# Normalised tiles 3 and 4 transposed by DMA in 16-bit halves, in a gated cross-attention and mixture kernel

## The reference

```
xn = layernorm(x)
x  = x + tanh(g_x) * (fake_quant(xn) @ fake_quant(ctx[b]))      # per batch b, ctx[b] is 1024 x 1024
z  = layernorm(x)                                               # "ln" in the kernel
gate = softmax(z @ W_gate.T);  thr = sigmoid(z @ W_thr + b_thr) * 0.125
w  = relu(gate - thr), divided by its sum
h  = z @ A_w.T                                                  # (rows, 8, 16)
x  = x + tanh(g_f) * (z @ W_base.T + b_base + 2 * (h * w) @ B_w)
```

## Time and profile before

| | us |
|---|---|
| median of 3 runs | 184.81 (184.8 to 185.39) |
| the profiled execution, its own time | 184.05 |
| its span, first to last instruction | 182.3 |

### The profile page before, as it was taken

The page is one execution under the profiler, slowest core; times in us unless marked ns, Lnnn a source line. Parts: engine busy times, 40 slices in busy tenths (PEclk is TensorE's granted clock), DMA queues, the critical chain, the costliest instruction groups (busy, mean ns, idle before and its releaser), DMA issues.

```text
span 182.3 us, 2890 instructions
## 1 busy us (share of the span) xinstructions
PE 172.4 (95%) x1052; PEld 149.9 (82%) x1058; DVE 111.9 (61%) x281; ACT 90.6 (50%) x123; POOL 72.0 (39%) x89
## 2 busy tenths in 40 slices
PE   4868999989999999999899999999999999999993
PEld 4755446678989999999764479999999999999993
DVE  0999985989678987968863563392451351351313
ACT  2389923575986936193910106142890880820300
POOL 3461023931001396199888887036400500500220
PEclk9999999999999999999999999999999999999999
DMA  6999999999130332065050000005309207102003
GB/s 210 318 381 386 386 410 406 362 395 387 62 117 0 112 118 119 0 117 174 0 169 7 0 0 0 4 0 101 129 0 150 84 0 171 61 4 115 2 0 115
DMA packets 19934, 25.39 MB, mean 139 GB/s; under 512 B 11207, under 2 KB 12615, under 8 KB 19920
## 3 DMA queue, kind: packets, MB, share of 16 engines
q1 hardware_dynamic: 19906, 25.21, 41.8%
q10 hardware_dynamic: 14, 0.00, 0.0%
HBM read 18.39 MB, written 4.19 MB: 124 GB/s over the span
## 4 chain that ended last, share of the span: by engine, by line
PE 76%; DVE 11%; DMA 4%; ACT 4%; issue 4%; POOL 0%; DVEq 0%; ACTq 0%
PE bank L1042 16%; PE bank L1044 16%; PE bank L1043 15%; PE bank L920 14%; PE bank L1002 3%; DVE st L661 3%; DVE q L696 2%; DMA q1T<-q 2%; PE bank L1066 2%; PE bank L978 2%; DMA xs<-in_x_dram 2%; PE bank L1068 2%; PE bank L1067 2%; DVE lnTl L729 1%; PE bank L1030 1%
## 5 line engine op out<-in xcount | busy, mean ns | idle before, releaser
L1042 PE MATMUL bank<-WTh,lnTh 128*128 128x388 f32 (+3 forms) x192 | 67.3, 350 | 0.3 <-DVE lnTl L729 0.3
L1044 PE MATMUL bank<-WTh,lnTl 128*128 128x388 f32 (+3 forms) x192 | 65.1, 339 | 0.0
L1043 PE MATMUL bank<-WTl,lnTh 128*128 128x388 f32 (+3 forms) x192 | 65.0, 339 | 0.0
L1042 PEld LDWEIGHTS bank<-WTh,lnTh 128*128 128x128 f32 x192 | 36.2, 188 | 1.2 <-DVE lnTl L729 0.6
L1043 PEld LDWEIGHTS bank<-WTl,lnTh 128*128 128x128 f32 x192 | 36.2, 189 | 0.3
L1044 PEld LDWEIGHTS bank<-WTh,lnTl 128*128 128x128 f32 x192 | 36.2, 188 | 0.3
L437 POOL TENSOR_TENSOR xs<-xs,tb 128x1024 f32<-128x1024 f32 x8 | 19.2, 2404 | 39.6 <-ACT xs L491 39.6
L920 PE MATMUL bank<-q,q1T 128*128 128x512 bf16 x122 | 29.1, 379 | 0.8 <-DVE q L696 0.5
L431 POOL TENSOR_TENSOR xs<-xs,colbc 128x512 f32<-128x512 f32 x14 | 18.0, 1309 | 15.9 <-DVE xs L715 11.1
L920 PEld LDWEIGHTS bank<-q,q1T 128*128 128x128 bf16 x128 | 12.1, 98 | 14.3 <-DVE q L696 0.6
L661 DVE BATCH_NORM_STATS2 st<-xs 128x6 f32<-128x512 f32 x32 | 20.7, 682 | 4.2 <-DMA xs<-in_x_dram 4.2
(11 more groups left out here) (102 smaller groups left out, 230.8 us busy)
## 6 DMA issues: line engine op xcount, KB each, us to landing
xs<-in_x_dram SPq DMA_DIRECT2D x8, 512.0 KB, 7.2
landing<-in_ctx_dram SPq DMA_DIRECT2D x8, 512.0 KB, 10.9
ring<-in_ctx_dram SPq DMA_DIRECT2D x8, 512.0 KB, 6.6
out_dram<-xs SPq DMA_DIRECT2D x7, 512.0 KB, 2.9
ring<-in_L_ffn_W_base_dram SPq DMA_DIRECT2D x4, 512.0 KB, 12.7
landing<-in_L_ffn_W_base_dram SPq DMA_DIRECT2D x4, 512.0 KB, 15.4
ring<-in_L_ffn_A_w_dram SPq DMA_DIRECT2D x1, 512.0 KB, 12.5
ring<-in_L_ffn_B_w_dram SPq DMA_DIRECT2D x1, 512.0 KB, 5.9
```

The costliest lines, as they stand in the source:

```text
L1042: mm(o, hi, WTh[:, k, a:b], start=(k == 0), stop=False, skip_group_check=True)
L1043: mm(o, hi, WTl[:, k, a:b], start=False, stop=False, skip_group_check=True)
L1044: ins = mm(o, lo, WTh[:, k, a:b], start=False, stop=(k == KT - 1), skip_group_check=True)
```

## The change

Tiles 3 and 4 are taken into `by_dma`: they are no longer transposed by TensorE but by DMA in halves. For tile 3 the transposed halves lie in `colbc`, which is free between the transposes of B and batch 1's column term, since slot 4 of the ring still holds ctx. Its `halve` stands behind `normalise(3)` in tile 1, its DMA ahead of batch 1's q1 transposes on SP, its join and high part behind the last ctx copies in tile 2, its low part among batch 1's additions. `halve(4)` stands behind `normalise(4)`. For tiles 4 to 7 the join stands behind the split of hw; before, it stood ahead of that split. The added wait in `transpose_ln`, for `flipped` of the second half of B, keeps the DMA off `colbc` until the transposes of B are done.

```diff
-    by_dma = [t for t in range(T) if t > MT]
+    by_dma = list(range(MT - 1, T))
...
-        halvesT = ring[:, 4, :].bitcast(U16).rearrange("p (b t) -> p b t", t=P)
+        def halvesT(t):
+            return (colbc[:, :] if t < MT else ring[:, 4, :]).bitcast(U16).rearrange("p (b t) -> p b t", t=P)
...
@@ SP, transpose_ln
                 if n:
                     sp.wait_ge(ln_joined, n)
-                sp.dma_start(halvesT, halves, transpose=True).then_inc(ln_transposed[t], 16)
+                else:
+                    sp.wait_ge(flipped, flip_no["B", 0, 1] + 1)
+                sp.dma_start(halvesT(t), halves, transpose=True).then_inc(ln_transposed[t], 16)
@@ SP, loop over t
                     if t + 3 == A1_AFTER:
+                        transpose_ln(MT - 1)
                         transpose_q1(MT)
                         transpose_q1(MT + 1)
                         transpose_q1(MT + 2)
                     if t + 2 == A1_AFTER:
                         transpose_q1(MT + 3)
-                    if t + 3 in by_dma:
+                    if t + 1 == A1_AFTER:
+                        transpose_ln(MT)
+                    if t + 3 in by_dma and t + 3 > MT:
                         transpose_ln(t + 3)
@@ ScalarE, loop over t
                 if t + 1 == MT:
                     normalise(MT)
+                    halve(MT)
...
-                if t + 1 in by_dma:
-                    join(t + 1)
-                elif t + 1 < T:
+                if t + 1 not in by_dma and t + 1 < T:
                     split_hi(("ln", t + 1, 0))
                     split_hi(("ln", t + 1, 1))
                 if t + 1 == A1_AFTER:
                     affine_ctx(CPB + 5)
                 split_hi(("hw", t, 0))
-                if t + 1 in by_dma:
+                if t + 1 in by_dma and t + 1 >= MT:
+                    join(t + 1)
                     joined_hi(t + 1)
...
-                if t + 2 in by_dma:
+                if t + 2 in by_dma and t + 2 != MT:
                     halve(t + 2)
...
                 if t + 1 == A1_AFTER:
                     affine_ctx(CPB + 6)
                     affine_ctx(CPB + 7)
+                    join(MT - 1)
+                    joined_hi(MT - 1)
                     scale_columns(1, 0)
                     scale_columns(1, 1)
@@ VectorE
                 split_lo(("hw", t, 0))
-                if t + 1 in by_dma:
+                if t + 1 in by_dma and t + 1 >= MT:
                     joined_lo(t + 1)
...
                     add_product(1, 0, 3)
+                    joined_lo(MT - 1)
                     add_product(1, 1, 0)
```

More of the change, by code:

```diff
@@ L536, in join @@
                 nc.scalar.copy(lnT.bitcast(U16).rearrange("p (c h) -> p h c", h=2),
-                               halvesT.rearrange("p (h k) t -> p h (k t)", h=2)).then_inc(ln_joined, 1)
+                               halvesT(t).rearrange("p (h k) t -> p h (k t)", h=2)).then_inc(ln_joined, 1)
             def joined_hi(t):
```

## The result

The changed kernel takes 190.54 us (median of 5 runs, 190.05 to 190.69) where the kernel before, run beside it, took 184.81: a ratio of 1.0302, 95% interval 1.0281 to 1.0322. Forecast were 189.6, in 187.8 to 191.2. The profiled execution, the fastest of the five, took 190.05 us with a span of 188.2, 5.9 above the span before.

What follows compares the result with a forecast made beforehand. TensorE, busy 95% of the span, bounds the kernel. Terms 0.0 + 3.25 + 0.74 + 0.74 = +4.7 us on the profiled 184.05 give 188.8; plus 0.76 for the median and 0.1 for first products, 189.6 us, range 187.8 to 191.2.

Steps and rivals of the forecast that it cites:

- tile 3 in sum: Tile 3 by DMA: -0.68 us for transposes gone from TensorE, +0.7 for q1's later landing, together 0.0.
- hw of tile 4 late: VectorE's moments wait behind tile 4's low part, so TensorE transposes hw of tile 4 2.51 us later than before.
- from there to tile 5: From hw of tile 4 to tile 5's first product: 5.48 us through the join instead of 4.74, +0.74.
- tile 6: Start of tile 6: TensorE waits for the join behind the split of hw, +0.74 us.
- tile 7: Start of tile 7: TensorE waits for the join behind the split of hw, +0.74 us.
- the queue on SP: Tile 3's transpose ahead of q1's on SP makes q1's data land late: 0.7 us taken, bounds 0 and 1.9.
- Tile 4's landing: DMA of tile 4's halves, issued at 112.1, lands before its join can start at 117.0, hidden by 0.1 to 0.7 us.
- the estimate set beside the sum: At some 275 ns per TensorE transpose, tile 4's eight would give back 2.2 us, whole sum about +3.3 us.
- The clock rival: TensorE's clock halves from the stop before hw of tile 4 to that tile's end: 194.3 us, chance 0.04.
- The rival of the joins alone: Only the late joins at tiles 4 to 7 cost, late moments being hidden: +2.1 us, 186.9 us, chance 0.06.
- the faster one: Join chain fits under 4.74 us and moments come under 1.28 us late: -1.55 us, 183.3 us, chance 0.04.
- The one of q1's transpose waiting out tile 3's: q1's data starts only after tile 3's landing, 2.1 us late: +6.1 us, 190.9 to 191.5 us, chance 0.10.

Runs made afterwards that it cites:

- experiment 2: Changed kernel with the join of tiles 5 to 7 ahead of the split of hw again, tile 4's join left behind it: 188.70 us.
- experiment 1: Changed kernel with VectorE's moments of tiles 5, 6 and 7 moved ahead of tile 4's low part: 187.62 us.
- experiment 4: Changed kernel with tile 4 back on TensorE and the joins of tiles 5 to 7 ahead of the split of hw: 185.01 us.
- experiment 6: Changed kernel with tile 3's DMA transpose issued on SP behind the q1 transposes of tiles 4 to 6: 189.97 us.
- experiment 7: Changed kernel, moments and joins of tiles 5-7 earlier, tile 3's transpose behind q1's, 16 idle start matmuls, earlier ctx rounding: 184.33 us; only tile 3 by DMA: 183.53.
- experiment 9: Kernel before with 16 idle start matmuls and earlier ctx rounding: 183.84 us; beside it, only tile 3 by DMA with all edits: 183.59 us.
- experiment 8: Changed kernel with 16 instead of 6 idle matmuls at its start: 189.91 us.
- experiment 3: Changed kernel with both the moments ahead of tile 4's low part and the join of tiles 5 to 7 ahead of hw's split: 185.06 us.

## Why the prediction was right

Against the spans of the two profiled executions, step by step in us:

| step | forecast | measured | from |
|---|---|---|---|
| granted clock at the start | none | +0.79 | hw split of tile 1: 72.25, 73.04 |
| tile 3 in sum | 0.0 | +0.15 | hw of tile 3: 116.56 forecast, 117.50 - 0.79 |
| hw of tile 4 late | +2.51 | +2.46 | 131.72, 135.12 - 0.79 - 0.15 |
| from there to tile 5 | +0.74 | +0.82 | 5.56 for 4.74 |
| tile 6 | +0.74 | +0.84 | 15.12 for 14.28 |
| tile 7 | +0.74 | +0.82 | 15.11 for 14.29 |
| sum | +4.73 | +5.88 | spans: +5.9 |

*The mechanism held where the time went.* The join behind the split of hw is too long by what the rows gave; experiment 2 removes the three starts. The moments queued behind tile 4's low part delay hw of tile 4 by 2.5 us, which swallows tile 4's own late start and the 0.87 us gained; experiment 1 takes exactly that stop away. Tile 3's added work was covered, and its transposes were no gain (experiment 4).

*Tile 3 came out for another reason than the one given, by luck.* The forecast was -0.68 for the transposes and +0.7 for the queue on SP, nothing behind. From the hw of tile 1 to that of tile 2 the changed kernel is 0.56 us faster (15.41 for 15.97), so most of the gain was there: the issue on SP took 1.93 us, q1's was issued hardly late, and experiment 6 puts the price of the queue at 0.26 to 0.28, which leaves 0.84 for the transposes, not 0.68. It was lost behind, from the hw of tile 2 to that of tile 3, 0.7 us, at a wait that was in no term of mine: TensorE stands 0.63 us for the column sum. VectorE and GpSimd around it:

```profile
93.64 1.47 DVE L706 TENSOR_SCALAR q<-q2u 128x1024 bf16<-128x1024 uint8 x1
...
92.17 2.39 POOL L428 TENSOR_TENSOR colacc<-colacc,q 128x512 f16<-128x512 f16 x2
95.19 5.49 POOL L428 TENSOR_TENSOR colacc<-colacc,q 128x512 f16<-128x512 f16 x4 [0.63 <-DVE q L706]
```

The same in the kernel before, with TensorE's row, which has no stop:

```profile
93.39 0.79 DVE L696 TENSOR_SCALAR q<-q2u 128x1024 bf16<-128x1024 uint8 x1
...
91.23 2.40 POOL L420 TENSOR_TENSOR colacc<-colacc,q 128x512 f16<-128x512 f16 x2 [0.63 <-DVE q L696]
94.26 5.48 POOL L420 TENSOR_TENSOR colacc<-colacc,q 128x512 f16<-128x512 f16 x4 [0.63 <-DVE q L696]
...
99.88 0.38 PE L986 MATMUL bank<-colacc,ones_h 128*128 128x512 f16 x1
```

The four additions end at 100.68 and TensorE goes on at 100.83; before, they ended at 99.74 and TensorE took the sum at 99.88. Less the 0.79 of the start, GpSimd is where it was, to 0.15 us. TensorE comes earlier by what tile 3 gave it, and finds GpSimd no earlier: before, it had been only just in time. The rounding on which the additions wait stands behind tile 2's last `finish`; moved ahead of it, TensorE's stop falls to 0.18 us (experiment 7, both tiles), and 0.25 us of tile 3's gain come out (experiment 9).

*Sizes that were off.* The late starts cost 0.82 to 0.84 rather than 0.74: the first product after a stop does not overlap the one before (0.41 us long instead of 0.34, the next one starting 0.25 us on instead of 0.18), for which I had 0.1 in all and not 0.1 each. Tile 4's landing was to be hidden by 0.1 to 0.7 us, with its DMA issued at 112.1; it was issued at 113.73, or 112.94 without the loss at the start, since `normalise(4)` waits for GpSimd's coefficients, which came that much later. In the profile that was just in time, in experiment 8 it was not. Two sums in the prediction are off without an effect: a slack of 1.28 us leaves out the 0.14 from VectorE's hw to TensorE (the 2.51 is reached with 1.14), and the estimate set beside the sum, with 2.2 us for eight transposes, comes to 4.73 - 1.33 = +3.4, not +3.3. The 275 ns that the prediction takes for it from the Trainium skill ("TensorE: Matmul & The Clock Gate", Part 4: PE-mode transpose) were measured for bf16, and the transposes here are of float32.

*What the forecast lacked.* The clock rival was given 0.04 and a price of 4.7 us. The fall does happen after that stop, in some executions (two of six in experiment 8), and costs 0.7: it lasts some 3 us and not to the end of the tile's work, and half of its loss falls into the wait for the join. It is not what lifts the median of the changed kernel: in experiment 2 the profile with both falls has a mean clock of 0.982, those with one fall have 0.990 or 0.991, and all five runs of the changed kernel have 0.990 or 0.991, which points to one fall each. The steps of the table without the clock make +5.09, the medians differ by 5.73. The 0.6 between stay open; a later landing at tile 4, as in experiment 8, could be 0.3 of them, which is not shown. The 0.76 us by which the median of before lay above its profiled execution, which I carried over as it was, fits the loss at the start: the profiled execution of before had the clock at 1.00, that of the changed kernel had not. For the three runs behind that median no clock is on record. If both medians carry this loss, that is why the forecast of the median was nearer than the table makes it look: +5.73 measured, +4.8 forecast.

The rival of the joins alone (+2.1) and the faster one (-1.55) are out, by experiments 1 and 4. The one of q1's transpose waiting out tile 3's is out too: its issue was late by 0.15 us against the rest (78.44 less 0.79, for 77.50).

## What to carry to other kernels

Moving work off the busiest engine helps only as far as the instruction that takes its place is not in front of something with less slack: here 0.87 us of transposes were exchanged for one low part, placed ahead of the moments, with some 1.1 us of slack behind them, and for a join placed behind the last event before it was needed. Before such a move, follow each new wait through the in-order queue of its engine to the next thing that the critical engine needs, and compare the delay with the slack there. A gain, too, holds only up to the next thing that comes no earlier, here GpSimd's column sum. And where a profile's time differs from the median, look at the granted clock of its first stages before a difference is given to the change.

## What the runs showed of the hardware

- The granted clock fell to its lower level (1.2 GHz) at 14 to 17 us in the changed kernel's profile, after a stop of TensorE of 1.75 us between short bursts, and it costs 0.8 us there; by the mean clocks this happens in about half of the executions of the kernel before. With ten more idle matmuls of 0.06 us each ahead of the stop the mean stayed at 0.999 or 1.000 in all twelve runs; in one profile the stop behind them was shorter (1.06 us for 1.53), in another it was not (1.85 us).
- With the clock granted at 1.00 eight 128x128 bf16 transposes took 1.03 us in one execution and 0.62 in another, at the same place behind a stop of 1.5 us (experiment 3 and before).
- The granted clock also fell after a single stop of 2.3 us in otherwise dense work, in some executions, for some 3 us; in others it stayed at 1.00 after the same stop. The Trainium skill ("TensorE: Matmul & The Clock Gate", Why this matters for your kernels) warns of gaps between bursts; these rows agree.
- The same VectorE rounding (128x1024 uint8 to bf16) took 0.79 us before and 1.47 us after. It had started 0.5 us earlier against the rest, and in both it ended 0.55 us after GpSimd's current addition did (93.39 + 0.79 = 94.18 and 91.23 + 2.40 = 93.63 before; 93.64 + 1.47 = 95.11 and 92.17 + 2.39 = 94.56 after). The Trainium skill ("SBUF — State Buffer", Terms) states that VectorE and GpSimd hold a shared pair of ports for a whole instruction, the other being blocked; these rows agree, and it was not tried by itself.
- A DMA transpose of 512 KB within SBUF landed 4.2 to 4.4 us after its issue in the changed kernel, and 4.3 to 4.6 in the last one with both tiles (experiment 7): a landing hidden by a few tenths is not hidden once the work ahead of it moves.
